# A graph network kernel: layer 1's last sums with two turn banks and four count copies, and the 25 diagonal blocks on GpSimd

## The reference

```python
h = max(layernorm(x), 0)
x = x + segment_sum((h @ W)[src] * edge_weight, dst) + bias          # layer 0
h = max(layernorm(x), 0)
agg = segment_sum(h[dst], src) / max(count(src), 1)                  # layer 1
out = relu(h @ Wl + bl + agg @ Wr + br)
x = x + out / (norm(out) + 1e-6)
...                                                                  # layers 2 and 3
```

## Time and profile before

| | |
|---|---|
| median of 3 runs | 2910.49 us (2902.32 to 2915.22) |
| the profiled execution | 2950.78 us, span 2949.0 us |
| granted TensorE clock, mean of the span | 0.748 |
| busy: TensorE, VectorE, ScalarE, GpSimd | 80%, 51%, 41%, 41% of the span |
| VectorE's 25 diagonal blocks (L763) | 704.8 to 709.9 us, 285 to 294 ns each |
| the last chunk's copies on ScalarE (L879, L882) | end at 672.6 us |
| the last sum's end, and the first load of the next stage | 736.8 and 737.9 us |

### The profile page before, as it was taken

One profiled execution on the slowest core, in us unless ns is written; L12 is line 12 of the kernel. 1 busy time (PEld: TensorE's weight loads), 2 busy tenths in 40 slices (PEclk: granted clock), 3 DMA queues, 4 the chain that ended last, 5 costly groups with the idle time before them and its releaser, 6 DMA issues.

```text
span 2949.0 us, 51575 instructions
## 1 busy us (share of the span) xinstructions
PE 2371.0 (80%) x12348; PEld 2007.6 (68%) x12453; DVE 1499.2 (51%) x6364; ACT 1215.3 (41%) x5336; POOL 1195.0 (41%) x1243
## 2 busy tenths in 40 slices
PE   2567676766518888888976889999998999999998
PEld 1444444542407787777853778788877888888887
DVE  4567666765515455455533555555564433333333
ACT  2556565653312233333321343434445444444443
POOL 3656566640056666666324665656642100000000
PEclk9977677776755555555568876757679999999999
DMA  3132313233333333333232333323336200000001
GB/s 84 51 103 54 104 52 106 56 94 86 87 96 83 91 92 92 92 92 91 69 85 76 89 90 87 94 76 91 92 87 251 74 26 22 23 23 23 23 23 55
DMA packets 177575, 227.46 MB, mean 77 GB/s; under 512 B 63568, under 2 KB 137625, under 8 KB 177145
## 3 DMA queue, kind: packets, MB, share of 16 engines
q0 software_dynamic: 50176, 131.74, 16.6%
q1 hardware_dynamic: 120286, 88.93, 10.0%
q10 hardware_dynamic: 6810, 3.40, 0.4%
HBM read 183.63 MB, written 40.29 MB: 76 GB/s over the span
## 4 chain that ended last, share of the span: by engine, by line
PE 59%; issue 13%; DVE 11%; another core or an unknown queue 7%; ACT 5%; ACTq 2%; SPq 1%; DMA 1%; POOL 1%; DVEq 0%; POOLq 0%
PE banks L2801 8%; PE banks L2797 8%; PE banks L1706 5%; PE banks L1767 4%; PE banks L1764 4%; PE banks L1765 4%; PE banks L850 3%; PE banks L1770 3%; PE banks L2803 2%; PE banks L2408 2%; PE banks L825 2%; PE banks L1768 2%; PE banks L828 2%; PE banks L841 1%
## 5 line engine op out<-in xcount | busy, mean ns | idle before, releaser
L231 POOL DMA_INDIRECT arena<-value_table,arena x392 | 395.3, 1008 | 387.6 <-DMA ed_table<-arena 169.3
L231 POOL DMA_INDIRECT arena<-gat_table,arena x392 | 394.3, 1006 | 360.4 <-PE banks L1770 184.1
L2797 PE MATMUL banks<-counts,u_parts 128*128 128x448 f32 x1323 | 491.9, 372 | 3.1 <-DVE u_parts L2930 3.1
L2801 PE MATMUL banks<-counts_even,u_parts 128*128 128x448 f32 x1323 | 487.1, 368 | 0.0
L231 POOL DMA_INDIRECT arena<-h_table,arena x392 | 375.4, 958 | 239.1 <-PE banks L828 128.7
L825 PE MATMUL banks<-arena 128*128 128x425 bf16 x392 | 184.8, 471 | 201.5 <-ACT arena L882 104.9
L2981 DVE CAST counts_even<-counts 128x448 fp32r<-128x448 bf16 x450 | 162.9, 390 | 303.9 <-PE banks L2801 275.4
L2797 PEld LDWEIGHTS banks<-counts,u_parts 128*128 128x128 f32 x1323 | 249.7, 189 | 23.9 <-ACT arena L2425 3.3
L1764 PE MATMUL banks<-arena 128*128 128x17 f32 x784 | 227.7, 371 | 46.0 <-issue 26.4
L2801 PEld LDWEIGHTS banks<-counts_even,u_parts 128*128 128x128 f32 x1323 | 249.8, 189 | 21.2 <-ACT counts_even L2905 0.3
L1764 PEld LDWEIGHTS banks<-arena 128*128 128x128 f32 x784 | 201.9, 319 | 54.4 <-issue 28.3
(11 more groups left out here) (286 smaller groups left out, 4883.5 us busy)
## 6 DMA issues: line engine op xcount, KB each, us to landing
adj_rows<-arena SPq DMA_DIRECT2D x4, 4000.0 KB
arena<-ed_table SPq DMA_DIRECT2D x784, 0.5 KB
arena<-turned_rows SPq DMA_DIRECT2D x27, 448.0 KB, 3.3
counts<-adj_rows SPq DMA_DIRECT2D x1, 7200.0 KB, 20.7
arena<-h_table,arena POOLq DMA_INDIRECT x392
arena<-value_table,arena POOLq DMA_INDIRECT x392
arena<-gat_table,arena POOLq DMA_INDIRECT x392
counts<-adj_rows SPq DMA_DIRECT2D x1, 5600.0 KB, 18.1
```

The source lines that it names most:

```text
L231: return e.indirect_dma_start(into, None, table, bass.IndirectOffsetOnAxis(ap=index.bitcast(U32), axis=0))
L2797: e.matmul(banks[:, 2 * r, 0:HALFW], weight, C_odd[:, w0:w0 + HALFW], start=start, stop=stop)
L2801: x = e.matmul(banks[:, 2 * r + 1, 0:HALFW], weight, tile(n), start=start, stop=stop)
```

## The change

Unit 150, called `LATE`, is the first whose slot lies four or more behind the last chunk (slot 396). From it on the turns go to bank 3 and bank 7 by turns (bank 3 belonged to the chunks), and the evictions to four copies by turns (two new ones in the words of the ring of gathered rows, which the chunks no longer need). The waits follow: the turn of u waits for the eviction of u-2, the eviction of u for the sum of u-4. The diagonal blocks leave VectorE's list; GpSimd makes them behind its last gather of the stage, by an addition of two SBUF operands, after one scaling of the identity. VectorE's degrees of blocks 23 and 24 move up to the slots 415 to 422.

```diff
+        LATE = next(u.i for u in UNITS if u.slot >= NC + 4)
...
+            CT += [at(late_at + k * QUAD * P // 2, [QUAD * P], BF16) for k in range(2)]
+            counts_of = lambda u: CT[u.i % 2] if u.i < LATE else CT[(2, 3, LATE % 2, (LATE + 1) % 2)[(u.i - LATE) % 4]]
+            turned_of = lambda u: banks[:, 7 if u.i < LATE or (u.i - LATE) % 2 else 3, :].bitcast(BF16)
...
+                e.wait_ge(l0_counted, NC)
+                e.wait_ge(l1_split, NB)
+                rows_stored(e)
+                small = at(loops_at - P // 2, [P], BF16)
+                pool_own.do(e.tensor_scalar(small, identb, SMALL, None, ALU.mult))
+                pool_own.settle(e)
+                for b in range(NB):
+                    x = e.tensor_tensor(LOOPS[:, b, :], small, C[:, b, b * P:(b + 1) * P], ALU.add)
+                x.then_inc(loops_made, 1)
...
-                degrees_from = {n.b: n.slot + 8 if n.b < NB - 2 else AFTER_SPLIT + 5 + 4 * (n.b - NB + 2) for n in NODES}
+                degrees_from = {n.b: n.slot + 8 if n.b < NB - 2 else AFTER_SPLIT + 4 * (n.b - NB + 2) for n in NODES}
...
-                    if c in loops_at_slot:
-                        loops(*loops_at_slot[c])
...
+                            if u.i == LATE:
+                                e.wait_ge(l0_acc, NC)
                             if u.i:
-                                e.wait_ge(l1_evicted, u.i)
+                                e.wait_ge(l1_evicted, u.i if u.i < LATE else u.i - 1)
...
                         if u.i >= 2:
-                            e.wait_ge(l1_product, u.i - 1)
+                            e.wait_ge(l1_product, u.i - 1 if u.i < LATE else u.i - 3)
```

More of the change, by code:

```diff
@@ L510, in build @@
         L0_at = CT_at + 2 * QUAD * P // 2
-        early_at = L0_at
+        late_at = L0_at
+        early_at = late_at + 2 * QUAD * P // 2
         indeg_in, odeg1 = at(into_at, [NPART, NB]), at(odeg_at, [NB])
@@ L774, in dve @@
                 assert len(degrees_at) == 3 * NB and len(degrees_added_at) == NB
-                loops_at_slot = {AFTER_SPLIT + k: (5 * k, 5 * k + 5) for k in range(NB // 5)}
                 total_at = {}
@@ L837, in pe @@
                             e.wait_ge(l0_acc, block_end(u.b))
+                            if u.i == LATE:
+                                e.wait_ge(l0_acc, NC)
                             if u.i:
-                                e.wait_ge(l1_evicted, u.i)
+                                e.wait_ge(l1_evicted, u.i if u.i < LATE else u.i - 1)
                             for s in range(n):
-                                x = e.transpose(banks[:, 7, :].bitcast(BF16)[:, s * P:(s + 1) * P], C[:, s0 + s, u.b * P:(u.b + 1) * P], identb)
+                                x = e.transpose(turned_of(u)[:, s * P:(s + 1) * P], C[:, s0 + s, u.b * P:(u.b + 1) * P], identb)
                             x.then_inc(l1_turned, 1)
@@ L849, in pe @@
                                     e.wait_ge(l1_agg, u.total - 1)
-                            x = e.matmul(banks[:, 5 + u.total % 2, 0:n * P], part_of(u.b, j), CT[u.i % 2][:, 0:n * P],
+                            x = e.matmul(banks[:, 5 + u.total % 2, 0:n * P], part_of(u.b, j), counts_of(u)[:, 0:n * P],
                                          start=u.begins and j == 0, stop=u.ends and j == 2, skip_group_check=True)
@@ L891, in act @@
                         if u.i >= 2:
-                            e.wait_ge(l1_product, u.i - 1)
-                        e.activation(CT[u.i % 2][:, 0:n * P], banks[:, 7, :].bitcast(BF16)[:, 0:n * P], ACT.Copy, scale=LARGE,
+                            e.wait_ge(l1_product, u.i - 1 if u.i < LATE else u.i - 3)
+                        e.activation(counts_of(u)[:, 0:n * P], turned_of(u)[:, 0:n * P], ACT.Copy, scale=LARGE,
                                      accum_out=indeg_in[:, u.q, u.b:u.b + 1]).then_inc(l1_evicted, 1)
```

## The result

The changed kernel takes 2899.11 us (median of 18 runs, 2879.25 to 2931.1), the kernel before 2926.11 us (18 runs, 2902.32 to 2953.53). The ratio is 0.9915 with a 95% interval from 0.9893 to 0.9938: faster by 18 to 31 us. The ratio is estimated from the single runs, without those over 1.5% above their kernel's fastest, and isn't the quotient of the two medians, 0.9908. The forecast was a ratio of 0.990 (2882 of 2910.5), which the interval holds. In microseconds the median lies 1.1 above the range, because the kernel before, too, has a median 15.6 us above the three runs that the forecast was scaled to.

A forecast was written before the change was run, and what follows sets the result against it. TensorE's serial loop of turn, eviction and sum was the bound. The later of sums (708.1) and store (707.7), plus 0.7, starts the next stage at 708.8 instead of 737.9; scaled, 28.6 off 2910.5 gives 2882 us, range 2873 to 2898.

The forecast's parts named there:

- Loop: Turn, eviction and sum from about 676 us: 0.92 us of TensorE idle time per 2.79 us round would go.
- Last split: VectorE's list from block 23's residual at 677.0 to the last `low`: at least 11.99 us, taken as 12.5, ending 689.5.
- Reductions ahead of the total of unit 162: Six reductions and an addition delay VectorE's total to 697.6; TensorE, at unit 165, stands some 5.5 us for it.
- Rest of the sums: TensorE from unit 165 on: 9.3 us from 697.7, with 4.8 us at half clock, so the last sum ends at 707.0.
- GpSimd and the store: 25 diagonal blocks at 0.411 us end at 701.0; their store takes 6.7 us and lands at 707.7, no longer covered.
- The stage: The loop's stretch up to the next stage's first load, which would come at 708.8 instead of 737.9: 29 us less.
- the 0.7 that the forecast had added for store and sums ending together: At the next stage's start: 0.7 us added because sums (708.1) and store (707.7) end close to each other.
- What follows has the same instructions and waits: Behind the changed stretch: instructions and waits stay the same; no further term was added for it.
- the base: Whole-kernel median 2910.5 us of the runs before, which the gain was scaled to (28.6 us) and taken off.
- The range: Whole-kernel time 2873 to 2898 us: cases 2881 to 2893, widened by the earlier runs' scatter, 8 below and 5 above.

The follow-up runs named there:

- ring_only: The changed kernel with diagonal blocks and degrees back in their old place in VectorE's list, leaving only new banks and copies; ratio 0.9924 to before, stage 33.12 us.
- addition_last: The changed kernel with the degrees' second addition moved behind the last total; 2891.94 us (one run), stage 33.27 us.
- reductions_between: The changed kernel with the reductions of blocks 23 and 24 spread between the totals, store still waited for; 2902.02 us (one run), stage 29.61 us.
- copies_only: The changed kernel with four copies but only one turn bank; 2927.42 us (one run), stage 40.09 us.
- gpsimd_only: The kernel before, with diagonal blocks on GpSimd and degrees moved up, banks and copies unchanged; ratio 0.9975 to before, stage 61.50 us.
- banks_only: The changed kernel with two turn banks but only the two old copies; 2918.69 us (one run), stage 36.99 us.
- after_again: The changed kernel once more, unchanged, timed beside the kernel before; 2904.57 us, ratio 0.9926, stage 36.25 us.

## Why the prediction held, and where it missed

**The mechanism held step by step.** Points in the order of the forecast:

- *Loop.* 0.87 us a round at full clock, for 1.96 at full and 2.79 at half; the idle time of the evictions is gone. Right.
- *Last split.* From the residual of block 23 (674.41 us after) to the end of the last `low` (686.74): 12.3 us, forecast 12.5. VectorE is busy for 11.14 of it, so its list takes up nearly all of the time, as forecast. The 11.99 us that the forecast took for a floor were no floor, since rows that follow closely overlap; but the waits came to 1.2 us and not 0.5, and the two errors cancel, which is luck. The window (columns as in rows 7):

```profile
674.41:686.74 12.33, 11.18 (x91) 6.37 (x90) 11.14 (x37) 8.38 (x29) 0.00 (x0) 1.00 0.55 157
```

- *Reductions ahead of the total of unit 162.* The total ends 8.3 us behind the split, forecast 8.1; TensorE stands 5.49, forecast 5.5. That wait, made by the new order, was worked out from rows 8 alone. That removing the blocks from VectorE is no saving of its own: shown by ring_only.
- *Rest of the sums.* From 695.15 to 705.91, 10.8 us, forecast 9.3. The clock did what was assumed (half, then full). Of the missing 1.5, 1.15 are the second stand, behind the second addition (2.29 us). It stands in the list ahead of the total of unit 164, and the forecast's sum has no term for it: its one addition, at about 0.1, is the first (0.40 measured). addition_last returns 0.93 of the stand.
- *GpSimd and the store.* A block started every 0.385 us; the forecast's 0.411 was the length of a row. The store landed 4.8 us behind the issue, forecast 6.7, which had been measured beside the loads of weights and h that SyncE's queue issued in the 5 us ahead of it. Both errors point the same way, so the store was done 5 us before the next stage's first load instead of level with the sums. reductions_between shows it as the next bound.
- *The stage.* 28.3 us, forecast 29.1. That it came so close is luck in part: the sums took 1.5 us more than forecast, but the 0.7 that the forecast had added for store and sums ending together wasn't needed. About 1 us more is given back behind the stage, since from the first load to the first gather it takes 87.8 us for 86.8. Most of it, 0.8 us, is there when TensorE begins its second group of products behind the h rows, 11.75 us after the first load for 10.95; the first of these groups took 3.9 us, at half clock to begin with, where before it took 2.5 at full clock. "What follows has the same instructions and waits" was true, but not its clock. Net 27.3.

**The step that failed is the base.** The forecast said that "the runs of before scatter by 8 below and 5 above their median", took the median of three, 2910.5, and read the profiled 2950.8 as 1.4% above the median. The three runs were the lowest, the second and the fourth of the 18 known now: the median is 2926.11, the scatter 24 below and 27 above, and 2950.8 lies within it. The three had been taken ahead of the other 15, whose median is 2929.64; three runs drawn from the 18 by chance would all be among the lowest four in only 4 of 816 cases, so something else than chance may have set them apart, and what it was stays open. Two more jobs give 2927.51 (23 runs) and 2928.37 (20 runs). With 2926 as base the same gain reads 2926 x 0.9902 = 2897.4, 1.7 below what was measured. The range was 25 us wide where single runs of one kernel span 51: it had the costs of the stage in it and, from three numbers, next to nothing for its own foundation.

**Where the scatter comes from.** The two profiles differ by 39.8 us of span, but the stage and what it gives back account for 27.3; the rest lies where the instructions are the same. In layer 2's second stage of gathers (of gat_table), copies_only and ring_only run the same 3344 matmuls in 675.70 and 651.10 us, at granted clocks of 0.71 and 0.75 (copies_only, then ring_only; windows):

```profile
1492.80:2168.50 675.70, 605.46 (x3344) 490.50 (x3342) 346.08 (x1666) 249.84 (x1438) 397.48 (x391) 0.71 0.33 87
```

```profile
1484.90:2136.00 651.10, 579.88 (x3344) 467.33 (x3342) 344.81 (x1663) 250.48 (x1435) 393.62 (x391) 0.75 0.34 90
```

One stretch moves by 24.6 us, almost the whole of what the change is worth. Over the 20 runs of before in the last job the time falls as the mean granted clock rises (correlation -0.81; 2910.05 us at 0.760, 2951.3 at 0.747). Whether the clock is the cause or follows from engines that wait differently in each run was not tried.

## What to carry to other kernels

Where a turn, an eviction and a product close into a loop over few buffers (here one bank and two copies), twice as many at either place open it, and most of the gain comes with the first of the two places; then look at once for what the new pace is late for, since here moving work off VectorE brought nothing beyond the ring until the reductions got a place between the totals. (Whether their new place would do as much with the diagonal blocks still on VectorE was not run.) Judge such a change in the trace, between two marks around the stage, and not by whole times that scatter more than it is worth. And before a forecast is scaled to a median, ask from how many runs it comes: a range has to hold the error of the base as well as that of the gain.

## What the runs showed of the hardware that had not been expected

A VectorE addition of two SBUF operands stood until GpSimd's whole row of additions was over. In the five traces that have GpSimd's blocks with the addition in its new place (the change and gpsimd_only above, banks_only, copies_only, after_again) it takes 2.29 or 2.30 us, against 0.18 or 0.19 with GpSimd idle, and each time it ends 0.04 us behind GpSimd's last block (in banks_only at 694.95 and 694.91, in copies_only at 699.99 and 699.95, in after_again at 694.43 and 694.39), over five blocks of 0.385 us after its start. The reductions, with one SBUF operand, were not held: three take 3.60 us beside GpSimd, against 3.70 before.

The Trainium skill, SBUF — State Buffer, section "SBUF: two separate sides", says that such a VectorE instruction and a GpSimd one that reads SBUF contend for one port pair under an exclusive lock: whichever starts first has it for its whole instruction, and the other is blocked meanwhile. The runs agree in who is held and who isn't, and the forecast used the rule in one direction only, for GpSimd behind VectorE. They differ in the length: 2.1 us of standing are more than five GpSimd instructions, not one, so by that rule VectorE did not get the ports between two of them. Yet the first addition, at 690.30 and also beside GpSimd, took 0.40 (0.40 or 0.41 in all five), which is a wait of at most one block, and in the trace of the change GpSimd's blocks went on starting every 0.38 us beside it. Why the one slipped in and the other didn't stays open.
